# Taking the memsets between groups of gathers out of a two-layer graph kernel, with its three-group holds left in

## What is computed

```python
h = jnp.maximum(_layernorm(x, axis=-1), 0.0)
x = x + _L0_gnn_ref(h, L0_gnn_weight, src, dst, edge_type_16)     # msg = h[src] @ weight[type]; summed by dst
h = jnp.maximum(_layernorm(x, axis=-1), 0.0)
x = x + _L1_gnn_ref(h, edge_index, edge_attr_8, W1, b1, W2, b2)   # msg = relu([h[src], h[dst], attr] @ W1 + b1) @ W2 + b2
return x
```

## Time and profile before

| | us |
|---|---|
| median of 3 runs | 4852.29 (4852.16 to 4860.69) |
| the profiled execution, its own time | 4855.4 |
| its span, first to last instruction | 4853.2 |
| POOL busy | 3380.0 (70%) |
| PE busy | 2787.7 (57%) |
| DVE busy | 1468.1 (30%) |
| ACT busy | 577.2 (12%) |

### The profile page before, as it was taken

One profiled execution on the slowest core, in us unless ns is written; L12 is line 12 of the kernel. 1 busy time (PEld: TensorE's weight loads), 2 busy tenths in 40 slices (PEclk: granted clock), 3 DMA queues, 4 the chain that ended last, 5 costly groups with the idle time before them and its releaser, 6 DMA issues.

```text
span 4853.2 us, 37713 instructions
## 1 busy us (share of the span) xinstructions
PE 2787.7 (57%) x10310; PEld 1549.3 (32%) x10310; DVE 1468.1 (30%) x2002; ACT 577.2 (12%) x1139; POOL 3380.0 (70%) x3742
## 2 busy tenths in 40 slices
PE   2565665656556655656565565565555655656555
PEld 1343343434334433434332232222222222222222
DVE  6322222222222222222232333233332332332333
ACT  3111111111111111111110010010000000100000
POOL 7567667666666666676757767777777777777776
PEclk9777776677767777776766666666666666666666
DMA  4111111111111111111111112111111111211111
GB/s 102 20 27 25 25 27 25 25 27 25 25 25 27 25 26 26 25 25 27 25 29 31 29 31 31 29 31 31 29 31 29 32 31 29 32 31 32 29 31 28
DMA packets 391187, 144.15 MB, mean 30 GB/s; under 512 B 321650, under 2 KB 337323, under 8 KB 391163
## 3 DMA queue, kind: packets, MB, share of 16 engines
q0 software_dynamic: 106304, 109.07, 11.8%
q1 hardware_dynamic: 282245, 34.18, 4.9%
q10 hardware_dynamic: 2614, 0.62, 0.1%
HBM read 129.03 MB, written 12.83 MB: 29 GB/s over the span
## 4 chain that ended last, share of the span: by engine, by line
POOL 39%; issue 26%; another core or an unknown queue 17%; PE 12%; DVE 3%; ACT 1%; SPq 1%; DMA 1%; POOLq 0%; DVEq 0%; ACTq 0%
POOL rows L710 36%; PE ps L1379 4%; PE ps L1386 2%; POOL spacer L763 2%; PE ps L1462 1%; PE ps L1461 1%; PE ps L1393 1%; POOL spacer L743 1%; PE ps L1344 1%; PE ps L1346 1%; DVE z_slot L1230 0%; PE ps L1466 0%; DVE q_blk L1243 0%; DVE slots L1219 0%
## 5 line engine op out<-in xcount | busy, mean ns | idle before, releaser
L710 POOL DMA_INDIRECT rows<-p_table,idx x1661 | 1579.6, 951 | 702.0 <-issue 631.3
L710 POOL DMA_INDIRECT rows<-h_table,idx x1533 | 1452.1, 947 | 693.8 <-issue 506.6
L1461 PE MATMUL ps<-w_attr,attr_t 64*128 64x512 f32 x416 | 400.9, 1063 | 1004.8 <-DVE q_blk L1243 694.7
L1379 PE MATMUL ps<-onehot,rows 128*64 128x256 f32 x3328 | 661.8, 512 | 101.2 <-DMA rows<-h_table,idx 50.8
L1386 PE MATMUL ps<-w_types,slots 128*128 128x128 f32 x3328 | 518.2, 307 | 226.5 <-issue 201.6
L1095 DVE TENSOR_TENSOR onehot<-key,ps 128x2048 f32<-128x2048 f32 x209 | 474.6, 2279 | 439.5 <-remote 389.5
L1386 PEld LDWEIGHTS ps<-w_types,slots 128*128 128x128 f32 x3328 | 462.3, 215 | 314.1 <-issue 282.5
L1219 DVE TENSOR_TENSOR slots<-ps,rows 128x512 f32<-128x512 f32 x208 | 143.9, 692 | 1378.1 <-DMA rows<-p_table,idx 831.5
L1379 PEld LDWEIGHTS ps<-onehot,rows 128*64 128x64 f32 x3328 | 333.6, 179 | 349.4 <-issue 287.8
L1461 PEld LDWEIGHTS ps<-w_attr,attr_t 64*128 64x128 f32 x416 | 96.8, 288 | 1041.8 <-issue 1041.4
L1462 PE MATMUL ps<-q_blk,onehot 128*128 128x512 f32 x416 | 422.2, 1118 | 0.0
(11 more groups left out here) (142 smaller groups left out, 1971.8 us busy)
## 6 DMA issues: line engine op xcount, KB each, us to landing
rows<-p_table,idx POOLq DMA_INDIRECT x1661
rows<-h_table,idx POOLq DMA_INDIRECT x1533
attr<-in_edge_attr_dram SPq DMA_DIRECT2D x52, 128.0 KB
q_win<-q_table SPq DMA_DIRECT2D x208, 32.0 KB
p_table<-pq_out SPq DMA_DIRECT2D x25, 120.0 KB
q_table<-pq_out SPq DMA_DIRECT2D x25, 120.0 KB
out_dram<-xs SPq DMA_DIRECT2D x25, 120.0 KB
xs<-in_x_dram SPq DMA_DIRECT2D x6, 480.0 KB, 6.4
```

The costliest lines, as they stand in the source:

```text
L710: pool.indirect_dma_start(rows[:, u, t, :], None, table, bass.IndirectOffsetOnAxis(ap=at, axis=0)).then_inc(s, 16)
L1379: last = pe.matmul(slot_ps[t % 2 * D:(t % 2 + 1) * D, b, t // 2, :], rows[:, u, t, :], onehot[:, b, t, :], start=True, stop=True)
L1461: pe.matmul(pre_ps[:, u % 2, :], attr_t[half, u // 2, :], w_attr[half].rearrange("k j d -> k (j d)"), start=True, stop=False)
```

## The change

The memset at the end of each group goes, with its tile, its semaphore and the wait for it, in both layers; the holds of three groups stay. Groups 16 to 23 (turn 2) are written out with groups 8 to 15 and read `src_tab` directly, so the loop of the first layer starts at turn 3, SP makes two copies to `idx` fewer, its store of chunk 0 stands ahead of its loop, and every later wait for `batch_in` counts one round less.

```diff
-        spacer = sb("spacer", [P, T * D], fp32)
...
-        spaced = sem("spaced")
...
-                with sp.Fori(2, NIT) as it:
+                store_pq(0, chunk_nodes)
+                with sp.Fori(3, NIT) as it:
                     for k in range(U // B):
                         batch(it, k)
                     store_pq(it - 2, chunk_nodes)
...
-                for u in range(U):
-                    pool.wait_ge(slots_summed, 2 * (AHEAD + u + 1))
-                    for t in range(T):
-                        gather(h_table, u, t, rows_in[u], of=U + u)
-                pool.sem_inc(spaced, 1)
-
-                def turn_of_rows(it, last=False):
+                def turn_of_rows(it, early=False, last=False):
                     for u in range(U):
-                        wait_apart(pool, spaced, (it - 2) * U + u + 1)
-
-                        if u % B == 0:
-                            wait_apart(pool, batch_in[u // B], 16 * (it - 1))
-                        wait_apart(pool, slots_summed, 2 * AHEAD + 2 * (it * U + u - 2))
+                        if not early and u % B == 0:
+                            wait_apart(pool, batch_in[u // B], 16 * (it - 2))
+                        if early and it == 1:
+                            pool.wait_ge(slots_summed, 2 * (AHEAD + u + 1))
+                        else:
+                            wait_apart(pool, slots_summed, 2 * AHEAD + 2 * (it * U + u - 2))
                         for t in range(SKIP if last and u == U - 1 else 0, T):
-                            gather(h_table, u, t, rows_in[u])
-                        pool.memset(spacer[:], 0.0).then_inc(spaced, 1)
-
-                with pool.Fori(2, NIT - 1) as it:
+                            gather(h_table, u, t, rows_in[u], of=it * U + u if early else None)
+
+                for it in (1, 2):
+                    turn_of_rows(it, early=True)
+                with pool.Fori(3, NIT - 1) as it:
                     turn_of_rows(it)
                 turn_of_rows(NIT - 1, last=True)
...
                 def turn_of_groups(it, last=False):
                     for u in range(U):
-                        wait_apart(pool, spaced, (NIT - 2 + it) * U + u + 1)
                         if u == 0:
                             wait_apart(pool, p_stored, 16 * (NC + 2))
                         if u % B == 0:
-                            wait_apart(pool, batch_in[u // B], 16 * (it + NIT - 1))
+                            wait_apart(pool, batch_in[u // B], 16 * (it + NIT - 2))
                         wait_apart(pool, pre_added, it * U + u + AHEAD - 2)
                         for j in range(SKIP if last and u == U - 1 else 0, T):
                             gather(p_table, u, j, rows_in[u])
-                        pool.memset(spacer[:], 0.0).then_inc(spaced, 1)
```

## The result

The changed kernel takes 5168.9 us (median of 4 runs, 5089.3 to 5195.1) against 4855.7 us before. The sign was forecast, the size was not: 4946 us was predicted, and the range ended at 5100.

What follows compares the result with a forecast made beforehand. POOL's gathers and memsets were taken to set the pace. 4855.4 + 34 (first layer) + 60 (second layer) = 4949.4 us; the median being 3.1 us lower, 4946 us was predicted, range 4640 to 5100.

Steps and rivals of the forecast that it cites:

- The sign: Whole kernel: slower, +1.9%, with a chance of 0.55 for slower against 0.39 for faster.
- Memsets out: Group ends, both layers: 400 memsets and their waits go, 1.20 us of POOL per group, leaving POOL's own pace 10.21 us.
- PE's signals come late while POOL runs: Both layers: during unbroken gathers PE's signals reach other engines only when POOL stops, so POOL pauses at the hold.
- Two groups per stall: Both layers: two groups go through per pause at the hold, 11.70 us per group before the first layer's node chunk.
- A pause at the hold costs 3.28 - 0.30 = 2.98 us: Holds of both layers: each pause of POOL costs 2.98 us beyond an ordinary step.
- groups 11 to 15: First-layer stretch without memsets, source of the pause price: POOL issues 16 gathers, then stands 3.28 and 3.22 us.
- First layer, half of today's 0.22 us for the node chunk: First layer: node-chunk work partly fits into the pauses; 11.81 us per group, +34 us in all.
- Second layer, two per pause: Second layer: two groups per pause because DVE and PE exchange several signals per group; 11.70 against 11.41 us, +60 us.
- Row numbers of groups 16 to 23, nothing: First layer, turn 2: written-out gathers and two fewer SP copies change nothing, 0 us.
- Gathers lengthened by VectorE, taken as 0: Both layers: gathers meeting DVE work on two SBUF inputs last 1.44 us, not 0.95; bound +51 us, taken as 0.
- the Trainium skill's rule: Rival: PE never waits, so POOL cannot hold it up and both layers run at POOL's own pace, 4333 us; chance 0.08.
- one stall per group at 2.98 us: Rival: second layer pauses at every group, 13.19 us per group, +368 in place of +60 us, 5254 us; chance 0.12.

Runs made afterwards that it cites:

- e1_tiny_memset: Kernel before with the memset cut to one column, its wait kept (break 0.75 us): 312 us of hold waits; total time not in the text.
- e2_wide_memset: Kernel before with the memset twice as wide (break 1.62 us): 15 us of hold waits; total time not in the text.
- e2_land: Changed kernel, POOL waiting at each group's end until its rows have landed: no step there over 5 us; total time not in the text.
- e4_qfirst: Changed kernel with a new second-layer order, Q picked ahead of the previous group's products and spread ahead of its addition: 5051.0 us, ratio 1.040.
- e1_rownum_only: Kernel before, memsets kept, with only the row numbers of groups 16 to 23 read straight from the on-chip table: 4856.1 us, ratio 0.9987.

## Why the prediction was wrong

- *Memsets out:* right. A step with no memset and no hold takes 1.25 us, and POOL's own pace is 10 us per group and a little. The wait on the hold with its counter, costed at nothing, costs nothing (the step from 3304.80 to 3306.05 above has it).
- *PE's signals come late while POOL runs, so a hold takes the place of the memset:* right, and the reason for the sign. e1_tiny_memset, e2_wide_memset and e2_land show it as a dose.
- *Two groups per stall:* near. 2.2 in the first layer, 2.8 in the second. At the forecast 2.98 us a stall, these counts would have made the kernel 25 us faster than forecast in the first layer and 88 us in the second.
- *A pause at the hold costs 3.28 - 0.30 = 2.98 us:* **this step failed.** It was read from groups 11 to 15, where POOL was released by the very signal that was late. In the first layer 67 of 87 stalls are of about that size, 3.27 us on average, and 56 of them end, as there, by an unmatched releaser; the other 20, each over 6 us, cost 9.34. In the second every stall ends by VectorE's addition; 29 cost 2.17 us on average and 45 cost 9.00. With 4.66 and 6.32 us in place of 2.98 the stalls cost 87 x 1.68 = 146 and 74 x 3.34 = 247 us more. In the long ones the late signal is an earlier link, and the chain behind it is walked from the start once the signal gets through: in the second layer the spread, the products and the addition.
- *First layer, half of today's 0.22 us for the node chunk, since part of that work fits into the pauses:* the same step, from the other side. In 15 of the 20 long stalls of this layer TensorE does work of the chunk (L1322, or L1337 and L1339) inside the stall. One of them, timelines of PE, ACT and POOL of the changed kernel:

```profile
1552.56 0.78 PE L1379 MATMUL ps<-w_types,slots 128*128 128x128 f32 x2 [0.34 <-issue]
...
1567.18 0.94 POOL L709 DMA_INDIRECT rows<-h_table,idx  x1 [0.30 <-issue]
...
1572.35 0.27 ACT L887 COPY nodes_t<-ps 128x128 f32<-128x128 f32 x1 [19.19 <-remote]
1572.59 0.59 ACT L836 COPY stage<-acc 64x480 f32 x1
1573.33 0.69 PE L1322 MATMUL ps<-ident,stage 64*120 64x64 f32 x4 [19.98 <-ACT stage L836]
...
1578.42 0.94 POOL L709 DMA_INDIRECT rows<-h_table,idx  x1 [10.29 <-PE ps L1372]
```

  The product ends at 1553.34 and ScalarE sees it 19.0 us later, 4.2 us after POOL stopped. Behind that copy in ScalarE's queue is the chunk's copy, TensorE waits for it in front of the next slot sums, and POOL waits for those: 6.1 us more. The forecast let the chunk run inside the pauses; it runs behind them.
- *Second layer, two per pause, because VectorE and PE must exchange several signals per group there:* the reason was right and was used for the count alone. The exchanges belong into the price of a stall: e4_qfirst takes one of them out and gets 111 us of the second layer back.
- *Row numbers of groups 16 to 23, nothing:* right (e1_rownum_only). *Gathers lengthened by VectorE, taken as 0:* right; inside the groups the steps add 16 us, where they added 51 before.
- *By the Trainium skill's rule in "SBUF — State Buffer", "Who interferes with whom", that PE and ACT never wait on anyone, the time would have been 4333 us:* the trace disagrees, 5169 us. That TensorE itself waits for SBUF is not shown by this, only that its signals are seen late; the ends of its matmuls are modelled in the profile.
- The range ended 69 us too low because its bounds were built from counts of stalls at one price; one stall per group at 2.98 us was the upper bound (5254 us with it in the second layer), most of which the range left out, and a price twice as high was not among the cases, though the row that gave the price came from another chain of waits than the second layer's.

What holds TensorE's signals up inside the chip stays open. By the runs, two signals in five fewer, no transposes and half the bytes leave most of the stalls, and POOL's standing still lets the signals through. Open is also why with the new order all 51 sums that ended 14 to 18 us after a break were late, and some that ended after 10 us, where that began at some 20 us: TensorE does more in that time, but leaving the transposes out did not move the limit.

## What to carry to other kernels

A memset or a wait that looks like dead time on the busiest engine can be what lets the other engines' signals through; before it is taken out, look in a stretch that has none of it at how long those signals take. And price a stall by the chain that starts when it ends: if the released signal is not the last link, the round trip behind it comes on top, once per stall. Deeper buffering need not help: with holds of eight groups the kernel took 5639 us.

## What the runs showed of the hardware

- While GpSimd issues indirect gathers back to back (one per 1.25 us), TensorE's signals are late. In the second layer of the changed kernel its sums are seen at once for some 18 us after a break and up to 16 us late from some 20 us on; with the new order they are late from 14 us on. VectorE's and ScalarE's own signals are not late (of those recorded none over 0.01 us).
- In the stall shown the late signals go up one at a time, some 5 us apart and in order, while the gathers run; the rest go up together some 5 us after the last gather. In the long stalls of the second layer the pick of Q gets through 3.54 and 5.29 us after it (medians, changed kernel and e4_qfirst).
- Breaks of 1.20 us per group of eight gathers (11% of GpSimd's time) leave 74 us of hold waits, 1.62 us (14%) 15, 0.75 us (7%) 312; the same 0.75 us twice per group (13%) some 80. Late signals in the second layer are gone at 13% and more, and at 10% with the new order.
- At a granted clock of 0.50, after 18.18 us of idle TensorE, two products took 4.04 us; at 1.00 they took 2.18.
- Chips differ: those of the changed kernel and of four series took 4855 to 4861 us for the kernel before, that of one 4953.
